# Loading the sorted messages of a graph layer's take pass from GpSimd's queue instead of SyncE's

## What is computed

```
edge_index = jnp.stack([src, dst])
x = _layernorm(x + _L0_gnn_ref(x, src, dst, edge_weight, W, b))
x = _layernorm(x + _L1_gnn_ref(x, edge_attr_8, Wq, Wk, Wv, Wo, src, dst))
x = _layernorm(x + _L2_gnn_ref(x, relvectors, w_ih, w_hh, b_ih, b_hh, src, dst, edge_type_16))
x = _layernorm(x + _L3_gnn_ref(x, edge_index, W1, b1, W2, b2, fc1_w, fc1_b, fc2_w, fc2_b))
```

```
msgs = edge_val[:, None] * X[edge_col]            # edge_col = dst
h = jax.ops.segment_sum(msgs, edge_row, num_segments=N_NODES)    # edge_row = src
return h @ W.T + b
```

## Time and profile before

| | |
|---|---|
| median of 3 runs | 4241.65 us (4234.1 to 4245.84) |
| the profiled execution | 4250.87 us |
| its span in the profile | 4249.1 us |
| TensorE's granted clock over the run | 0.826 of full speed |
| busy: PE, DVE, ACT, POOL | 3247.8, 2354.5, 961.5, 1504.2 us |
| G<-tab_m, issued by SP | 448 DMAs of 129.0 KB, 2.2 us from issue to landing |

### The profile page before, as it was taken

How to read it: one execution, slowest core, us unless ns; L and a number is a source line. 1 busy time by engine, 2 the same in 40 slices (tenths; PEclk the granted TensorE clock), 3 DMA queues, 4 the chain that set the end, 5 groups by cost and what they waited for, 6 DMA issues and landing times.

```text
span 4249.1 us, 69189 instructions
## 1 busy us (share of the span) xinstructions
PE 3247.8 (76%) x12167; PEld 1997.0 (47%) x12169; DVE 2354.5 (55%) x8003; ACT 961.5 (23%) x2857; POOL 1504.2 (35%) x1736
## 2 busy tenths in 40 slices
PE   1106777767778877777887888887777799999998
PEld 1103444434446434334775666655333366555754
DVE  5606666644443577776557888887777600254002
ACT  0002222210003222221112444442355200154000
POOL 0006777740000477774004666672000022100443
PEclk6558888879999898996555788887678899999999
DMA  2122222236651344434001333332133255200887
GB/s 85 35 20 82 101 100 101 100 104 178 174 139 44 84 106 106 106 105 69 0 0 56 91 94 94 94 96 28 69 125 128 92 150 145 88 1 7 279 263 235
DMA packets 338898, 422.23 MB, mean 99 GB/s; under 512 B 182634, under 2 KB 256560, under 8 KB 338518
## 3 DMA queue, kind: packets, MB, share of 16 engines
q0 software_dynamic: 94512, 295.27, 23.5%
q1 hardware_dynamic: 208024, 120.68, 10.3%
q10 hardware_dynamic: 36238, 4.74, 0.8%
HBM read 312.03 MB, written 112.79 MB: 100 GB/s over the span
## 4 chain that ended last, share of the span: by engine, by line
PE 42%; DVE 14%; issue 12%; POOL 11%; DMA 11%; ACTq 3%; ACT 2%; SPq 2%; DVEq 2%; POOLq 0%
PE PSA L822 12%; POOL G L404 9%; DMA tab_m<-G,posi 7%; PE PSA L950 7%; PE PSA L786 6%; PE PSA L809 4%; PE PSA L930 3%; DVE S L1489 3%; ACTq L450 2%; PE PSA L943 2%; PE PSA L1005 2%; DVE S L1490 1%; POOL tab_m L394 1%; PE PSA L840 1%; DMA G<-tab_m 1%
## 5 line engine op out<-in xcount | busy, mean ns | idle before, releaser
L840 PE MATMUL PSA<-ident,oh 128*128 128x128 f32 x1344 | 450.8, 336 | 321.1 <-DVE oh L1213 315.4
L568 ACT COPY ohT<-PSA 128x128 f32<-128x128 f32 x1344 | 355.0, 264 | 1335.7 <-PE PSA L840 1276.4
L404 POOL DMA_INDIRECT G<-tab_k,srci x448 | 424.7, 948 | 644.4 <-DMA tab_v<-KV 508.2
L404 POOL DMA_INDIRECT G<-tab_v,srci x448 | 436.7, 975 | 479.4 <-PEq L954 277.2
L394 POOL DMA_INDIRECT tab_m<-G,posi x448 | 436.3, 974 | 470.8 <-DVE G L1244 436.7
L422 POOL DMA_DIRECT2D G<-tab_A x375 | 201.5, 538 | 1106.3 <-PE PSA L822 637.7
L840 PEld LDWEIGHTS PSA<-ident,oh 128*128 128x128 f32 x1344 | 216.5, 161 | 641.1 <-DVE oh L1213 586.4
L950 PE MATMUL PSA<-work,oh 128*128 128x280 f32 x896 | 396.5, 531 | 68.1 <-DVE work L1418 45.2
L1213 DVE TENSOR_SCALAR oh<-iota_f,dstl 128x128 f32<-128x128 f32 x1344 | 410.8, 306 | 7.7 <-PE PSA L786 4.7
L849 PE MATMUL PSA<-X,ohT 128*128 x896 | 355.0, 487 | 50.6 <-DVE G L1242 42.1
L899 PE MATMUL PSA<-Q,ohT 128*128 x896 | 354.5, 485 | 39.7 <-ACT ohT L568 29.8
(11 more groups left out here) (297 smaller groups left out, 4798.5 us busy)
## 6 DMA issues: line engine op xcount, KB each, us to landing
G<-tab_A POOLq DMA_DIRECT2D x375, 320.0 KB, 3.6
G<-tab_m SPq DMA_DIRECT2D x448, 129.0 KB, 2.2
tab_A<-G SPq DMA_DIRECT2D x125, 320.0 KB, 2.1
WT<-tab_m SPq DMA_DIRECT2D x544, 1.0 KB
tab_m<-G,posi POOLq DMA_INDIRECT x448, 2.5
G<-tab_k,srci POOLq DMA_INDIRECT x448, 2.8
G<-tab_v,srci POOLq DMA_INDIRECT x448, 2.7
rec<-tab_rec ACTq DMA_DIRECT2D x224, 6.5 KB, 1.8
```

The source lines that it names most:

```text
L404: pool.indirect_dma_start(G[:, t % GR, :p.w], None, p.table, bass.IndirectOffsetOnAxis(ap=srci[:, t:t + 1], axis=0)).then_inc(p.rows[t % G ...
L568: act.copy(ohT[:, r % 4, :], PS[r % 2][:, 0:P]).then_inc(s_(name + "_ohTc"), 1)
L840: pe.transpose(PS[r % 2][:, 0:P], oh[:, r, :], ident[:, :]).then_inc(s_(name + "_ohT"), 1)
```

## The change

The loop of L484 to L490 leaves SP's program and stands in POOL's, between the scatters of the send pass and the gathers of the keys pass. `loaded` is moved up so that POOL's program can call it. The pass's semaphores are now the first 8 of the 16 `ROWS`, so the bases of all passes are counted per semaphore in the order send, take, keys, vals; the stores of `tab_A` get 4 semaphores of their own that count from 0.

```
-        for n, p in enumerate((pm, pk, pv)):
-            p.base = 16 * (T // GR) * n
-        p0.ring, p0.rows, p0.base = U, [sem(f"taken{u}") for u in range(U)], 0
-        ab_in, b_out = ROWS[0:NA], p0.rows
-        out_base = 16 * (T // U)
-        in_base = [16 * (T // GR) * 3] * NA
+        p0.ring, p0.rows = U, ROWS[0:U]
+        landed = [0] * GR
+        for p in (pm, p0, pk, pv):
+            p.base = list(landed)
+            for r in range(p.ring):
+                landed[r] += 16 * (T // p.ring)
+        ab_in, in_base = ROWS[0:NA], landed[0:NA]
+        b_out, out_base = [sem(f"stored{k}") for k in range(SLOTS)], 0
...
         @block.gpsimd
...
+            for r in range(GR):
+                pool.wait_ge(pm.rows[r], 16 * (T // GR))
+            with pool.Fori(0, TURNS) as i:
+                first = loaded(ET.Pool, as_row[1], Step(i * U, 0), E)
+                for u in range(U):
+                    pool.wait_ge(p0.used, i * U + (u + 1 + AHEAD - U))
+                    pool.dma_start(G[:, u, 0:MW], tab_m[bass.ds(first[u], P), :]).then_inc(p0.rows[u], 16)
+
             def gathers(p, ready, count):
...
         @block.sync
...
-            for r in range(GR):
-                sp.wait_ge(pm.rows[r], 16 * (T // GR))
-            with sp.Fori(0, TURNS) as i:
-                first = loaded(ET.SP, as_row[1], Step(i * U, 0), E)
-                for u in range(U):
-                    sp.wait_ge(p0.used, i * U + (u + 1 + AHEAD - U))
-                    sp.dma_start(G[:, u, 0:MW], tab_m[bass.ds(first[u], P), :]).then_inc(p0.rows[u], 16)
...
-                    pe.wait_ge(p0.rows[r], p0.base + t // U * 16 + 16)
+                    pe.wait_ge(p0.rows[r], p0.base[r] + t // U * 16 + 16)
...
-                dve.wait_ge(p0.rows[r], turn * 16 + (p0.base + 16))
+                dve.wait_ge(p0.rows[r], turn * 16 + (p0.base[r] + 16))
```

More of the change, by code:

```diff
@@ L363, in settle, with loaded @@
             eng.sem_inc(passed, 1)
+        def loaded(eng, row, t, most):
+            _, values = nc.values_load_multi_w_load_instructions(column(row, t, 1, 0, U), engines=[eng],
+                                                                 bass_reorder=False)
+            return [v.with_bounds(min_val=0, max_val=most) for v in values]
         @block.gpsimd
@@ L426, in _ @@
             chunks(2)
[L428 to L432, removed]
         class Tiles:
@@ L1312, in product @@
                 dve.wait_ge(s_("keys_sel"), t + (1 + U))
-                dve.wait_ge(pk.rows[r], turn * 16 + (pk.base + 16))
+                dve.wait_ge(pk.rows[r], turn * 16 + (pk.base[r] + 16))
                 dve.wait_ge(s_("keys_red"), t + 1)
@@ L1416, in weigh @@
                 dve.wait_ge(s_("vals_e"), t + 1)
-                dve.wait_ge(pv.rows[r], turn * 16 + (pv.base + 16))
+                dve.wait_ge(pv.rows[r], turn * 16 + (pv.base[r] + 16))
                 dve.tensor_tensor(work[:, r % 4, 0:D].rearrange("p (h d) -> p h d", h=H),
```

## The result

| | before | after |
|---|---|---|
| median of 4 runs each | 4243.74 us (4234.1 to 4249.51) | 4292.03 us (4276.6 to 4295.54) |
| the profiled execution | 4250.87 us | 4276.6 us |
| its span | 4249.1 us | 4275.0 us |
| first to last load of the take pass | 334.3 us, 5.97 a turn | 365.7 us, 6.53 a turn |

The ratio is 1.0109, with a 95% interval of 1.0078 to 1.014: the kernel became slower by 33 to 59 us, where 42 us less had been forecast. The take pass grew by 31.4 us, and the forecast had named a pass of over 322 us as what would make it fall.

The account below looks back on a forecast made before the run. SP's issue work was taken to bound the take pass; on POOL, 56 turns of 5.2 us make 291 us instead of 334.3, -43, and +1 for landings and waits: 4241.65 - 42 = 4200 us, range 4165 to 4300.

Parts of the forecast that it names:

- What bounds the kernel now: Take pass: SP's issue work alone is 96% of it, 5.97 us a turn over 56 turns.
- First, the issue: POOL's plain load in the take pass: 0.54 us each, against SP's 333 ns; bounds 0.33 and 1.25 us.
- Second, the register work: POOL's sequencer in the take pass runs ahead, hiding 3.1 us of its own work beside 4.3 us of issue a turn.
- The first rival: POOL does its register work in line between loads and at loop's end: 8.5 us a turn, +144 us, chance 0.10.
- The slots: G's 8 slots in the take pass: landing and reuse set 5.2 us a turn, between 4.6 and 5.75.
- The consumers: DVE and PE in the take pass: 8 tiles at 0.475 us plus PE's 1.1 us register load, 4.9 us a turn.
- The landing: Take-pass load from issue to arrival: 2.2 us from SP, 2.8 to 3.6 taken for POOL.
- rival 3: Take pass: a landing of 4.1 to 4.5 us takes the whole gain, 4230 to 4255 us, chance 0.14.
- Rival 2: POOL's descriptors cost over 0.746 us a tile; +226 us as indirect, +61 taking turns with DVE; chance 0.10.
- Costed at nothing: Renamed semaphores, their bases and four new store semaphores: the same waits with other constants, 0 us.
- Nothing is queued behind it: POOL between last scatter and first gather: it idles there, so the added loop delays nothing queued later.
- The sum: Take pass 291 us instead of 334.3, -43; +1 for landings and waits; -42 in all, giving 4200 us.

Follow-up runs that it names:

- e9: e2 with SP's loop in 28 turns of 16 tiles instead of 8, still 8 slots; 4231.32 us, ratio 0.9942 to before.
- e2: The changed kernel with the load loop back on SP, its semaphore counting and four new store semaphores kept; 4254.48 us, ratio 1.0 to before.
- e7: The changed kernel with even tiles loaded by SP and odd ones by POOL, 8 slots, turns of 8 tiles; 4224.92 us, ratio 0.9921 to before.
- e10: e5 with 16 slots and VectorE's take-pass loop over 16 tiles; 4135.73 us, ratio 0.9722 to before.
- e5: e4 with every load reading the first 128 rows of tab_m, so no register work; 4211.43 us, ratio 0.9899 to before.
- e4: The changed kernel with POOL's loop written out, no branch and waits on constants; 4246.2 us, ratio 0.9979 to before.
- e8: e7 with 16 slots, turns of 16 tiles on each queue and VectorE's loop over 16; 4127.28 us, ratio 0.9699 to before.
- e1: The changed kernel run again without any edit; 4297.8 us, ratio 1.0104 to before.
- e11: e2 (loads on SP, 8 slots) with only VectorE's take-pass loop over 16 tiles instead of 8; 4229.12 us, ratio 0.9943 to before.
- e12: The changed kernel (loads on POOL, 8 slots) with only VectorE's take-pass loop over 16 tiles instead of 8; 4256.69 us, ratio 1.0019 to before.
- e3: The changed kernel with POOL's loop in 28 turns of 16 tiles, still 8 slots; 4277.46 us, ratio 1.0061 to before.
- e6: e3 with 16 slots of G and VectorE's take-pass loop over 16 tiles; 4235.6 us, ratio 0.995 to before.

## Why the prediction was wrong

- **"What bounds the kernel now": right.** SP's issue work was the bound. Halving SP's loop ends alone made the pass 17 us shorter (e9 against e2) and the kernel 0.6% faster; with the queue's work shared out, the pass fell to 293 us (e7).
- **"First, the issue", 0.54 us: right as the instruction's duration** (536 ns in 448 loads), and rows of 1032 and 2560 bytes indeed cost the same. But it was read as the time of a part that works behind the sequencer.
- **"Second, the register work": the step that failed.** I costed POOL's 0.26 us per load and 1.0 per turn at nothing, because the MOVE at 345.9 had passed beside a scatter. A load takes the queue for 0.527 us even where its instruction lasts 1.04 us and overlaps the next (e10). What is put between two loads adds to it: 0.07 us for the two register instructions of the address (e5's 0.527 to e4's 0.597), 0.07 for the one of the wait (e4's to after's 0.666), 0.94 at the loop's end. A turn is 8 x 0.666 + 0.94 = 6.26 us and not 4.3, and so above what SP needs. The MOVE in the earlier trace rows was true, but of a scatter of 0.97 us. That a scatter of this length leaves room for a sequencer that needs less is my guess; no kernel tried it. The six loads of tab_A in 3.29 us had the same 0.55 us, and I took it for the descriptors' time; they tell nothing of a loop with registers, for they have none.
- **The first rival was what happened, at a lower price.** Its point of decision, 0.62 us a tile with 1.0 at the loop's end, was right: 0.666 and 0.94 are above it, by little, and the loss is small. Its own price, 0.94 us a tile and +144 us, was too high, since it added the indirect loads' 0.30 us of idle time, which the plain ones don't have. The 0.55 us of the earlier trace rows and SP's 0.26 for register work would have made it 0.81 a tile, 7.5 a turn and +85. The register work turned out cheaper on POOL, two steps of 0.07 instead of 0.26, and with these it is 0.69 a tile, 6.5 a turn and +31. The pass grew by 31.4, but so near a hit is partly luck: this sum leaves out the four stalls (10 us) and some 5 us of short waits in after, and the 15 us by which before's pass exceeds 56 turns of 5.7.
- **"The slots", 5.2 us a turn: right as a number** wherever the queue is quick enough. e5 (292.8) and e7 (292.9) stand at it, against the 291 us forecast. Its terms weren't: I had gone towards a landing of 3.6 us, and e5's is 2.6, which with the 1.7 for the rest would have made 4.3 a turn. No run shows what takes the other 0.9 us of the circle, so the number was met partly by luck. In after it hardly came to bear.
- **"The consumers", 4.9 us a turn: too high.** e8 does 4.1. In the rows before, PE's register load of 1106 ns was taken as a stop of that length each turn; in e8 the matmuls stop for 0.45 us per turn, and 16 of them run in 3.72.
- **The landing**, between 2.2 and 2.8 us: 2.5, so rival 3 (4.1 to 4.5 us) fell. The Trainium skill, DMA: Bandwidth & Descriptors, section "Specifications", puts the first byte at about 1 us from GpSimd's queue and 0.6 from SP's, 0.4 us apart. The rows show landings and not first bytes, and these are 0.3 us apart.
- **Rival 2, POOL and DVE taking turns, fell.** DVE's one-hot takes 346 ns at the median beside POOL's loads, as it did beside SP's (row by instruction of after):

```profile
L1264 DVE TENSOR_SCALAR oh<-iota_f,G,offs x448: 340/346/441, 917.1 to 1284.5; 128x128 f32<-128x128 f32 x150
```

353 of after's 448 loads overlap a one-hot in time; they take 536 ns at the median, as do the 95 that overlap none. The loads are 0.666 us apart and not 0.88. The Trainium skill (SBUF — State Buffer, section "SBUF: two separate sides") has the lock for DVE instructions in a two-port mode. No run shows whether the one-hot runs in such a mode: if it does, the trace disagrees with the rule, and if it doesn't, the rule says nothing of this kernel.
- **"Costed at nothing", the semaphores: right as far as tried** (e2, 1.0). "Nothing is queued behind it" held too.
- **The sum.** Of the 48 us between the medians, 31 are the pass. The other 17 are not settled: in e1 too some 19 us lie outside the pass, but the intervals of both begin at 28 to 33 us, where the pass alone would put them, and the vals pass swings by more than that between executions. The two profiled executions differ by 25.9 us of span, less than their passes; and between e11 and e12 nothing is left outside the pass. What a clock-bound pass does after a change elsewhere was no term of my sum.

The time lies inside the range, close to its upper end of 4300 us, but that end had been set by rival 2's cheap part and not by what happened. The sign was wrong, since a single row, of another kind of DMA, decided the step that carried two thirds of the chance.

## What to carry to other kernels

A queue is priced by what its sequencer does between two DMAs, register instructions, waits and the loop's end included, and not by the DMA instruction's busy time; a burst of DMAs without registers is only the lower bound of a loop with them. Before moving loads from a queue that is the bound to another, compare both per turn (here 5.7 and 6.26 us), and consider sharing the loads out: two queues that each issue half, with slots enough for both, took 3% off where moving them all cost 1%. Of these 3%, by e11, some 0.6% may belong to VectorE's longer loop and not to the shared loads. When a change's time goes beyond the stage that it touches, check the granted clock of the later stages before a cause is sought in it.

## What the runs showed of the hardware

- Plain loads of 128 rows from GpSimd's queue, where nothing stands between them, start 0.527 us apart at the median, with instructions of 536 ns in e5 and overlapping ones of 1042 ns in e10. On SP the issue instruction is 333 ns, and 0.59 us with the register work. The Trainium skill, DMA: Bandwidth & Descriptors, section "Issuing engines are not separate DMA queues", says that issuing from several engines saves only the sequencer's time for the initiation, usually small beside the DMA. By e7 and e8 that time is what is saved, and here it isn't small: it set the length of the pass.
- POOL stalls at regular places. In after the next load starts 3.25 us and not 0.67 us after the 113th, the 219th, the 325th and the 431st, so every 106 loads, and in e1, e3, e4 and e12 at the same counts (3.2 to 3.5 us). In e6 it is after the 57th, 155th, 253rd and 351st, so every 98 loads, and 3.06 us. In e10 no distance is over 1.1 us, but the only two over 0.7 us (1.02 and 1.05) come after the 155th and the 253rd load. The cause wasn't found, and no kernel was made for it.
- The vals pass, with the same instructions, took 598 to 660 us in these profiles, at granted clocks from 0.92 to 0.69 of 2.4 GHz, shorter on the whole the higher the clock. VectorE's loop of 16 tiles in the take pass went with the short end in four of five kernels that have it. With a change of 1%, a swing of this size can hide or double what is measured.
